# Audio tower on one core: the loads that lay out queries and keys move from SyncE's queue to GpSimd's

## Chip, cores and metric

The kernel runs on one core of a Trainium2 chip. The metric is the device time of one execution in microseconds, the median of the runs shown. The engines are TensorE (PE), ScalarE (ACT), VectorE (DVE), GpSimd (POOL) and SyncE (SP, which here only issues DMAs).

## What is computed

Eight waveforms of 120,000 samples are cut into frames of 80, so that each gives S = 1500 tokens of width D = 256. Each token goes through a layer of weights, a layer norm and an exact GELU, then through self attention with 16 heads of width 16 and a residual. In a last layer, tokens are routed to heads with an attention of their own, added, and normed once more; both kernels leave out this routed attention (its weights are no inputs of theirs) and compute the norm of that layer and its residual. What matters here:

```python
def proj(W, b):
    return (x @ W.T + b).reshape(B, S, H, hd).transpose(0, 2, 1, 3)
Q, K, V = (proj(Wq, bq), proj(Wk, bk), proj(Wv, bv))
scores = jnp.einsum('bhqd,bhkd->bhqk', Q, K) * scale
attn = jax.nn.softmax(scores, axis=-1)
out = jnp.einsum('bhqk,bhkd->bhqd', attn, V)
```

## The kernel before

**Units and periods.** The attention is done in 96 units, 12 to a batch: four groups of four heads, times three chunks of 500 queries. A unit has 24 periods, numbered from 0. In a period TensorE makes the scores of two heads for one tile of 125 keys (`scores`, L972), ScalarE takes their exponential as one instruction of 1000 columns (L537), and TensorE multiplies by the values in every second period (`attend`, L1002). The scores run one period ahead of the exponentials, in two pairs of PSUM banks. In each odd period TensorE also does one step of other work (`beside`): tokens of the next batch (`tok`), transposes (`turn`), projections to queries or keys (`qk`, four steps, L894), values (`val`), sums of squares (`norm`, L933), the test of the scores' range (`flag`) or the output projection (`out`, L924). The table PLAN names unit and period of each; NORMS names (4, 12), (5, 12) and (6, 8) for the layer norm of the next batch. Every engine walks the same loop over units and periods, and its instructions stand in that order; semaphores alone hold it in step with the others.

**The way of a projection.** A `qk` step number i (0 to 11 of a batch; even for queries, odd for keys) ends in PSUM. VectorE writes it as two halves of 16 bits into HL (L619, L621). `store_halves` sends HL to a scratch in HBM by one DMA on SP's queue (L281, 250 KB). GpSimd squares the upper half (`squares`, L426) for the range test. `lay_out` (L285 to L296) waits for the store (semaphore s_st) and issues eight DMAs of 62.5 KB on SP's queue (L295), which put the rows of the heads where the scores read them, in QA or KA. TensorE waits for all 48 DMAs of six projections (`laid_out`, on s_ld) before the first scores of unit 0 and of unit 6 of a batch, and these first scores stand in period 23 of the unit ahead. In the plan, projections end in period 9, 13 or 23; `lay_out` follows three periods after the store, so most of them stand in period 2 of the next unit.

**What else stands on SP's queue.** For the unit before, each unit issues three small steps: in period 1 `spread_sums` (thin<-Osb, L300), in period 7 `gather_sums` (Den<-thin, L304), in period 12 `store_attended` (oT<-Osb, L315). Between them VectorE inverts (L675) and multiplies (L679, L681). In period 13 come the loads of x and the stores of the output (out<-Y, L321, 500 KB).

**What stands on GpSimd.** `root1` (L402, L404) for the tokens, `root2` (L408, L410) and `add_bias` (four passes, L418) for the layer norm ahead of the projections, `squares` (L426), and `out_root` (L433 to L437) for the last layer norm. Who waits for them: VectorE for the roots, in `tok_norm` (L583), `norm_apply` (L600) and `finish_out` (L702, three periods after `take_out`); TensorE in `norm_sums`, which reads two squares and stands in period 3 of units 1, 3, 5, 7 and 9 and once in unit 10. The one in period 3 of unit 5 reads the squares of projections 10 and 11, and projection 11 ends in period 23 of unit 4.

Ahead of the first unit the same steps are done for six projections of batch 0, and `lay_out` follows each store on SP.

Of the kernel before, what the change touches and what calls it, by code (L numbers as in the profile page):

```python
# [5 lines left out]
def audio_tower(nc, x, tok_wT, tok_b, tok_g, tok_be, wqT, bq, wkT, bk, wvT, bv, woT, bo, ln_g, ln_b, out):  # L6
# [9 lines left out]
    HD = D // H  # L16
    QC = 500
    NC = S // QC
# [10 lines left out]
    WIN = NT * HG // 2  # L29
# [128 lines left out]
    with ExitStack() as ctx:  # L158
# [92 lines left out]
        def at(sem_, count):  # L251
            return count + TOTAL.get(sem_, 0) if second[0] else count
# [3 lines left out]
        def nth(b, i):  # L256
            return 12 * b + i

        def chunk_of(i):
            return i % (2 * NC) // 2  # L260
# [10 lines left out]
        def _(sp):  # L271
# [8 lines left out]
                sp.wait_ge(s_free, at(s_free, USE["qk", b, i] + 1))  # L280
                sp.dma_start(qk_s[b, i, :, :, :], HL[:, p % 3, :, :]).then_inc(s_st[p % 3], 16)  # L281

            def lay_out(b, i):  # L285
                p, k, w, m = nth(b, i), chunk_of(i), i % 2, i // (2 * NC)
                dst = KA if w else QA
                sp.wait_ge(s_st[p % 3], at(s_st[p % 3], 16 * (p // 3 + 1)))
                if p >= 4 * NC or second[0]:
                    sp.wait_ge(s_sc, at(s_sc, max(0, WIN * NC * 2 * (p // (2 * NC) - 1))))  # L290
                for par in range(2):
                    for blk in range(4):
                        to, half_ = 64 * par + HD * blk, blk // 2 if w else blk % 2
                        src = qk_s[b, i, :, half_, :].rearrange("(a two r) q -> two r a q", two=2, r=HD)
                        sp.dma_start(dst[to:to + HD, 2 * m:2 * m + 2, :, k * QC:(k + 1) * QC], src[par])\  # L295
                          .then_inc(s_ld, 16)  # L296

            def spread_sums(n):
                sp.wait_ge(s_ov, at(s_ov, n + 1))
                sp.dma_start(thin[:, :], Osb[HD:128:2 * HD, :].rearrange("j (s c) -> j s c", s=25)).then_inc(s_pk, 16)  # L300
# [22 lines left out]
            def run():  # L323
                load_x(1)
                for i in range(2 * NC):
                    store_halves(0, i)
                    if i > 0:
                        lay_out(0, i - 1)
                lay_out(0, 2 * NC - 1)
                stored = []  # L330
                for n in range(B * NU):
                    b, u = n // NU, n % NU
                    for k in range(WIN):
                        if stored and stored[0][0] == WIN * n + k:
                            lay_out(*stored.pop(0)[1:])
                        if k == TAKE and n > 0:
                            spread_sums(n - 1)
                        if k == INVERT and n > 0:
                            gather_sums(n - 1)
                        if k == NORMALISE and n > 0:  # L340
                            store_attended(n - 1)
                        if k == NORMALISE + 1:
                            if u == 4 and b + 2 < B:
                                load_x(b + 2)
                            if u in (1, 3, 6) and b > 0:
                                store_out(b - 1, u // 2 if u < 6 else 2)
                        for what, pb, i, step, last in pieces(b, u, k):
                            if what == "qk" and last:
                                store_halves(pb, i)
                                stored.append((WIN * n + k + 3, pb, i))  # L350
                spread_sums(B * NU - 1)
                gather_sums(B * NU - 1)
                store_attended(B * NU - 1)
                store_out(B - 1, 0)
                store_out(B - 1, 1)
                store_out(B - 1, 2)
# [27 lines left out]
        def _(pool):  # L384
# [27 lines left out]
            def add_bias(b, k):  # L412
                pool.wait_ge(s_z, at(s_z, b * NC + k + 1))
                if b == 0 and k == 0:
                    pool.wait_ge(s_wo, 16 * 5)
                for e in range(k * CT, k * CT + CT):
                    h = Hs[:, hslot(b, e), :]
                    ins = pool.tensor_tensor(h, h, b_o[:, :], ALU.add)  # L418
                ins.then_inc(s_hb, 1)

            def squares(b, i):
                p = nth(b, i)
                pool.wait_ge(s_free, at(s_free, USE["qk", b, i] + 1))
                if p >= 2:
                    pool.wait_ge(s_nm, at(s_nm, p // 2))
                pool.tensor_tensor(sq[:, p % 2, :], HL[:, p % 3, 0, :], HL[:, p % 3, 0, :], ALU.mult).then_inc(s_sq, 1)  # L426

            def out_root(b, e):
                n, k = b * NT + e, b * NC + e // CT
                if e % CT == 0 and k >= 2:  # L430
                    pool.wait_ge(s_yst[k % 2], at(s_yst[k % 2], 16 * (k // 2)))
                pool.wait_ge(s_free, at(s_free, USE["out", b, e] + 1))
                pool.tensor_tensor(Y[:, k % 2, e % CT, :], Hs[:, hslot(b, e), :], be_ln[:, :], ALU.add)  # L433
                pool.wait_ge(s_s1, at(s_s1, n + 1))
                pool.tensor_scalar(rs3[:, n % 2:n % 2 + 1], mv3[:, n % 2, 1:2], 1.0 + EPS, EPS * EPS, ALU.mult, ALU.add)
                pool.drain()
                pool.tensor_tensor(rs3[:, n % 2:n % 2 + 1], rs3[:, n % 2:n % 2 + 1], mhalf[0:T, 0:1], ALU.pow)\  # L437
                    .then_inc(s_r3, 1)

            def run():  # L440
                for i in range(NT // 2):
                    root1(0, i)
                    if i == 1 and not second[0]:
                        pool.wait_ge(s_top, 1)
                        pool.tensor_tensor(root[:, :], top[:, :], half[:, :], ALU.pow).then_inc(s_root, 1)
                root2(0, 0)
                for k in range(NC):
                    if k + 1 < NC:
                        root2(0, k + 1)
                    squares(0, 2 * k)  # L450
                    squares(0, 2 * k + 1)
                for k in range(NC):
                    add_bias(0, k)
                for b in range(B):
                    for u in range(NU):
                        for k in range(WIN):
                            if b + 1 < B and (u, k) in NORMS:
                                root2(b + 1, NORMS[u, k])
                                add_bias(b + 1, NORMS[u, k])
                            for what, pb, i, step, last in pieces(b, u, k):  # L460
                                if what == "tok" and last:
                                    root1(pb, i)
                                if what == "out" and last:
                                    out_root(pb, i)
                                if what == "qk" and last:
                                    squares(pb, i)
                for e in range(CT + 1, NT):
                    out_root(B - 1, e)

# [689 lines left out]
```

## Time and profile before

| | |
|---|---|
| median of 3 runs | 2360.52 us (2359.71 to 2369.72) |
| profiled execution | 2361.47 us |
| its span, first to last instruction | 2359.7 us |
| mean granted TensorE clock | 0.966 |
| busy: ACT / PE | 2134.5 us (90%) / 2080.5 us (88%) |
| busy: DVE / POOL | 963.5 us (41%) / 394.8 us (17%) |
| first exponential starts | 89.49 us |

The span is 1.8 us shorter than the execution's own time. ScalarE is busy for nine tenths of the span, and the exponentials are nearly all of that. A rise of time therefore shows as idle time of ScalarE between two exponentials. In the answers of the trace times are microseconds from the start of the span. A row of a timeline has start, duration, engine, line, operation, tiles, count, and in brackets the idle time of the engine ahead of it and what ended it.

### The profile page before, as it was taken

The numbers are of one execution on the slowest core, as the hardware profiler recorded it, in microseconds if no ns is written. First come the engines' busy times: TensorE is split into PE (matmuls) and PEld (weight loads), VectorE is DVE, ScalarE is ACT, GpSimd is POOL, SyncE is SP. The second block draws the span as 40 slices with busy tenths as digits, with TensorE's granted clock in tenths as the row PEclk, the third lists the DMA queues.
The fourth block names the chain that finished last, engine by engine and source line by source line (L and its number), as shares of the span: only waits on it lengthen the run. The fifth ranks groups of instructions, "written<-read, shape, count | busy, mean of one in ns | idle before, by whom it ended". The sixth has DMA issues, their size and how long they took to land.

```text
span 2359.7 us, 123320 instructions
## 1 busy us (share of the span) xinstructions
PE 2080.5 (88%) x56576; PEld 902.7 (38%) x56576; DVE 963.5 (41%) x2261; ACT 2134.5 (90%) x2334; POOL 394.8 (17%) x637
## 2 busy tenths in 40 slices
PE   4798999889998899988999799998999889999885
PEld 1432444333433344433444344443444333433223
DVE  6443335452344424444345433454335453343214
ACT  1498999989999899998999899998999989999993
POOL 2211102130122201222012210222102130011003
PEclk7998999999999999999999999999999999999997
DMA  2311211212121120221212112121211203122001
GB/s 71 81 45 42 56 42 46 56 31 75 32 57 48 44 67 22 59 64 43 62 25 57 53 48 58 35 58 38 66 41 48 53 23 78 28 58 57 18 10 35
DMA packets 114866, 113.91 MB, mean 48 GB/s; under 512 B 41003, under 2 KB 110698, under 8 KB 114338
## 3 DMA queue, kind: packets, MB, share of 16 engines
q1 hardware_dynamic: 111802, 104.10, 17.3%
q8 instruction: 446, 7.31, 1.3%
q10 hardware_dynamic: 2536, 1.83, 0.3%
q14 instruction: 82, 0.67, 0.1%
HBM read 55.16 MB, written 36.86 MB: 39 GB/s over the span
## 4 chain that ended last, share of the span: by engine, by line
ACT 40%; PE 27%; issue 13%; DVE 7%; SPq 5%; DMA 4%; POOL 2%; DVEq 2%; POOLq 0%
ACT prob L537 39%; PE PS L1002 12%; PE PS L972 7%; SPq L295 3%; DMA qk_halves_scratch<-HL 3%; PE PS L924 2%; SPq L315 1%; PE PS L871 1%; PE PS L909 1%; PE PS L894 1%; DMA oT<-Osb 1%; DVE Hs L576 1%; DVE z L600 1%; DVE Den L679 1%; POOL Hs L418 1%
## 5 line engine op out<-in xcount | busy, mean ns | idle before, releaser
L537 ACT ACTIVATE prob<-PS 125x1000 f32<-125x1000 f32 x2304 | 2089.7, 1070 | 155.9 <-PE PS L972 151.2
L1002 PE MATMUL PS<-prob,Vst 64*17 64x500 f32 (+1 forms) x18432 | 1214.7, 587 | 1.6 <-issue 0.8
L972 PE MATMUL PS<-QA,KA 64*32 64x500 f16 (+1 forms) x18432 | 958.9, 381 | 132.4 <-ACT prob L537 124.5
L972 PEld LDWEIGHTS PS<-QA,KA 64*32 64x32 f16 (+1 forms) x18432 | 276.8, 90 | 1054.0 <-ACT prob L537 1004.2
L1002 PEld LDWEIGHTS PS<-prob,Vst 61*17 61x17 f32 (+1 forms) x18432 | 341.3, 93 | 42.2 <-issue 9.0
L619 DVE TENSOR_SCALAR HL<-PS,b_qk 128x500 f16<-128x500 f32 x96 | 70.9, 739 | 459.4 <-PE PS L894 453.2
L894 PE MATMUL PS<-zT,w_qk 64*32 64x250 f32 x5760 | 229.4, 372 | 15.0 <-DVE Hs L576 8.5
L426 POOL TENSOR_TENSOR sq<-HL 128x500 bf16<-128x500 f16 x96 | 98.1, 1022 | 861.1 <-DVE HL L621 761.1
L924 PE MATMUL PS<-w_o,oT 64*32 64x128 f32 (+1 forms) x6144 | 129.9, 279 | 38.7 <-DVE Hs L576 27.9
L433 POOL TENSOR_TENSOR Y<-Hs,be_ln 125x256 f32<-125x256 f32 x96 | 70.3, 732 | 540.3 <-DVE Hs L688 529.5
L909 PE MATMUL PS<-w_v,zT 64*32 64x128 f32 (+1 forms) x5376 | 116.9, 280 | 34.2 <-DVE nrow L643 33.6
L894 PEld LDWEIGHTS PS<-zT,w_qk 64*32 64x32 f32 x5760 | 107.5, 106 | 70.8 <-DVE Hs L576 12.1
L924 PEld LDWEIGHTS PS<-w_o,oT 64*32 64x32 f32 (+1 forms) x6144 | 99.8, 108 | 88.6 <-DVE Hs L576 41.5
L909 PEld LDWEIGHTS PS<-w_v,zT 64*32 64x32 f32 (+1 forms) x5376 | 91.8, 109 | 66.2 <-DVE nrow L643 36.8
L688 DVE TENSOR_TENSOR Hs<-Hs,PS 125x256 f32<-125x256 f32 x96 | 40.3, 420 | 186.9 <-PE PS L924 186.9
L669 DVE COPY Osb<-PS 128x500 f32<-128x500 f32 x96 | 64.5, 672 | 117.9 <-PE PS L1002 116.4
L628 DVE TENSOR_TENSOR Vst<-PS,b_v 125x256 f32<-125x256 f32 x96 | 39.8, 419 | 160.4 <-PE PS L909 159.5
L871 PE MATMUL PS<-w_tok,X 40*32 40x256 f32 (+3 forms) x1536 | 68.2, 405 | 13.6 <-DMA w_tok<-in_tok_b 9.5
L418 POOL TENSOR_TENSOR Hs<-Hs,b_o 125x256 f32<-125x256 f32 x96 | 71.5, 775 | 31.4 <-DVE z L600 31.4
L675 DVE RECIPROCAL thin<-thin 100x20 f32<-100x20 f32 x96 | 26.5, 276 | 119.8 <-DMA thin<-Osb 119.8
L621 DVE SCALAR_TENSOR_TENSOR HL<-PS,b_qk,HL 128x500 f16<-128x500 f32 x96 | 71.0, 739 | 7.5 <-issue 0.4
L681 DVE TENSOR_TENSOR Osb<-Den,Osb 128x500 f32<-128x500 f32 x96 | 68.3, 712 | 7.5 <-issue 0.4
(83 smaller groups left out, 968.9 us busy)
## 6 DMA issues: line engine op xcount, KB each, us to landing
qk_halves_scratch<-HL SPq DMA_DIRECT2D x96, 250.0 KB, 2.3
QA<-qk_halves_scratch SPq DMA_DIRECT2D x384, 62.5 KB
KA<-qk_halves_scratch SPq DMA_DIRECT2D x384, 62.5 KB
oT<-Osb SPq DMA_DIRECT2D x384, 31.2 KB, 2.0
out<-Y SPq DMA_DIRECT2D x24, 500.0 KB
X<-in_x SPq DMA_DIRECT2D x16, 234.4 KB
thin<-Osb SPq DMA_DIRECT2D x96, 7.8 KB
Den<-thin SPq DMA_DIRECT2D x96, 7.8 KB
```

The lines of the kernel that those rows point to most:

```text
L295: sp.dma_start(dst[to:to + HD, 2 * m:2 * m + 2, :, k * QC:(k + 1) * QC], src[par])\
L418: ins = pool.tensor_tensor(h, h, b_o[:, :], ALU.add)
L426: pool.tensor_tensor(sq[:, p % 2, :], HL[:, p % 3, 0, :], HL[:, p % 3, 0, :], ALU.mult).then_inc(s_sq, 1)
L537: act.activation(prob[0:T, 2 * (w % 6):2 * (w % 6) + 2, :], PS[0:T, 2 * (w % 2):2 * (w % 2) + 2, 0:QC], ACT.Exp, scale=scl)\
L619: dve.tensor_scalar(hi, both, bias, None, ALU.add)
L621: dve.scalar_tensor_tensor(out=lo, in0=both, scalar=bias, in1=hi, op0=ALU.add, op1=ALU.subtract)\
L871: last = pe.matmul(PS[lo:hi, bank + j, 0:D], X[rows, 2 * i + j, lo:hi], w_tok[rows, :], start=(step == 0), stop=(step == 1))
L894: last = pe.matmul(PS[lo:hi, bank + j, 0:QC // 2], w_qk[rows, c, w, m * 128 + lo:m * 128 + hi], zT[rows, c, k * QC + j * QC // 2:k * QC + ...
L909: last = pe.matmul(PS[lo:hi, bank + j, 0:D // 2], zT[rows, c, t + lo:t + hi], w_v[rows, c, j * D // 2:(j + 1) * D // 2], start=(step == 0 ...
L924: last = pe.matmul(PS[lo:hi, bank + j, 0:D // 2], oT[rows, c, oslot(b, e // CT), e % CT * T + lo:e % CT * T + hi], w_o[rows, c, j * D // 2 ...
L972: last = pe.matmul(PS[lo:hi, bank, 0:QC], KA[rows, G % NG, h // 2, t * T + lo:t * T + hi], QA[rows, G % NG, h // 2, c * QC:(c + 1) * QC], ...
L1002: last = pe.matmul(PS[lo:lo + HD + 1, bank + r, 0:QC], Vst[rows, b % 2, t, g * HG + j, :], prob[rows, (HG * t + j) % 12, :], start=(t == 0 ...
```

## The change

`lay_out` is the same function with the same eight DMAs and the same waits, but it stands in GpSimd's program and issues on GpSimd's own queue. SP's program loses it. Its place in GpSimd's order: ahead of the first unit, after the two squares of each chunk; later in period 13 (`NORMALISE + 1`), ahead of that period's other pieces, where all projections that were stored so far and are not yet laid out are taken. A projection that ends in period 23 is thus laid out in period 13 of the next unit, one that ends in period 9 in period 13 of the same unit, and one that ends in period 13 of unit 6 in period 13 of unit 7.

```diff
@@ SyncE
-            def lay_out(b, i):
-                ...
-                sp.wait_ge(s_st[p % 3], at(s_st[p % 3], 16 * (p // 3 + 1)))
-                ...
                 for i in range(2 * NC):
                     store_halves(0, i)
-                    if i > 0:
-                        lay_out(0, i - 1)
-                lay_out(0, 2 * NC - 1)
-                stored = []
...
-                        if stored and stored[0][0] == WIN * n + k:
-                            lay_out(*stored.pop(0)[1:])
...
-                                stored.append((WIN * n + k + 3, pb, i))
@@ GpSimd
+            def lay_out(b, i):
+                p, k, w, m = nth(b, i), chunk_of(i), i % 2, i // (2 * NC)
+                dst = KA if w else QA
+                pool.wait_ge(s_st[p % 3], at(s_st[p % 3], 16 * (p // 3 + 1)))
+                if p >= 4 * NC or second[0]:
+                    pool.wait_ge(s_sc, at(s_sc, max(0, WIN * NC * 2 * (p // (2 * NC) - 1))))
+                for par in range(2):
+                    for blk in range(4):
+                        to, half_ = 64 * par + HD * blk, blk // 2 if w else blk % 2
+                        src = qk_s[b, i, :, half_, :].rearrange("(a two r) q -> two r a q", two=2, r=HD)
+                        pool.dma_start(dst[to:to + HD, 2 * m:2 * m + 2, :, k * QC:(k + 1) * QC], src[par])\
+                          .then_inc(s_ld, 16)
...
                     squares(0, 2 * k)
                     squares(0, 2 * k + 1)
+                    lay_out(0, 2 * k)
+                    lay_out(0, 2 * k + 1)
...
                         for k in range(WIN):
+                            if k == NORMALISE + 1:
+                                while stored:
+                                    lay_out(*stored.pop(0))
                             if b + 1 < B and (u, k) in NORMS:
...
                                 if what == "qk" and last:
                                     squares(pb, i)
+                                    stored.append((pb, i))
```

The lines of the changed kernel are numbered anew: its `squares` is L404, `root2` is L386 and L388, `add_bias` L396, `out_root` L426 to L430 and the DMAs of `lay_out` L418. On SP the store of HL is still L281, the spread, gather and attended DMAs are L285, L289 and L300.

**GpSimd ahead of the first unit**, before (sq is the tile of squares, rs of the roots, Hs of the tokens):

```order
L426 TENSOR_TENSOR sq<-HL 128x500 x2
L408 TENSOR_SCALAR rs<-mv 125x4
L410 TENSOR_TENSOR rs<-rs,mhalf 125x4
L426 TENSOR_TENSOR sq<-HL 128x500 x4
L418 TENSOR_TENSOR Hs<-Hs,b_o 125x256 x12
```

and now:

```order
L404 TENSOR_TENSOR sq<-HL 128x500 x2
L418 DMA QA<-qk_halves_scratch 16x4x500 x8
L418 DMA KA<-qk_halves_scratch 16x4x500 x8
L386 TENSOR_SCALAR rs<-mv 125x4
L388 TENSOR_TENSOR rs<-rs,mhalf 125x4
L404 TENSOR_TENSOR sq<-HL 128x500 x2
L418 DMA QA<-qk_halves_scratch 16x4x500 x8
L418 DMA KA<-qk_halves_scratch 16x4x500 x8
L404 TENSOR_TENSOR sq<-HL 128x500 x2
L418 DMA QA<-qk_halves_scratch 16x4x500 x8
L418 DMA KA<-qk_halves_scratch 16x4x500 x8
L396 TENSOR_TENSOR Hs<-Hs,b_o 125x256 x12
```

All 48 DMAs now stand on GpSimd, 16 of them ahead of the root of the third chunk's norm, and the squares lie between them.

**GpSimd in units 4 and 5 of a batch**, from the norm in period 12 of unit 4 to the end of the one in unit 5, now (without the two rows of DMAs it is the order before, with the other line numbers):

```order
L386 TENSOR_SCALAR rs<-mv 125x4
L388 TENSOR_TENSOR rs<-rs,mhalf 125x4
L396 TENSOR_TENSOR Hs<-Hs,b_o 125x256 x4
L418 DMA QA<-qk_halves_scratch 16x4x500 x8
L404 TENSOR_TENSOR sq<-HL 128x500
L426 TENSOR_TENSOR Y<-Hs,be_ln 125x256
L428 TENSOR_SCALAR rs<-mv 125x1
L430 TENSOR_TENSOR rs<-rs,mhalf 125x1
L386 TENSOR_SCALAR rs<-mv 125x4
L388 TENSOR_TENSOR rs<-rs,mhalf 125x4
L396 TENSOR_TENSOR Hs<-Hs,b_o 125x256 x4
L418 DMA KA<-qk_halves_scratch 16x4x500 x8
```

The first eight DMAs (projection 10) stand between the bias of unit 4 and the square of projection 11; the second eight (projection 11) behind the bias of unit 5.

**SP around the start of unit 7**, before:

```order
L281 DMA qk_halves_scratch<-HL 128x1000
L295 DMA QA<-qk_halves_scratch 16x4x500 x8
L281 DMA qk_halves_scratch<-HL 128x1000
L300 DMA thin<-Osb 100x1x20
L295 DMA KA<-qk_halves_scratch 16x4x500 x8
L304 DMA Den<-thin 4x25x20
L315 DMA oT<-Osb 16x500 x4
```

and now:

```order
L281 DMA qk_halves_scratch<-HL 128x1000 x2
L285 DMA thin<-Osb 100x1x20
L289 DMA Den<-thin 4x25x20
L300 DMA oT<-Osb 16x500 x4
```

The second store and the two DMAs of the sums no longer have sixteen DMAs and two waits for stores among them.

## Rows read from the trace of the kernel before

**Rows 1.** The page, its first part: busy time, share, instructions of each engine.
```profile
PE 2080.5 (88%) x56576; PEld 902.7 (38%) x56576; DVE 963.5 (41%) x2261; ACT 2134.5 (90%) x2334; POOL 394.8 (17%) x637
```

**Rows 2.** Groups by line: count | busy us, mean ns | idle before, releaser.
```profile
L537 ACT ACTIVATE prob<-PS 125x1000 f32<-125x1000 f32 x2304 | 2089.7, 1070 | 155.9 <-PE PS L972 151.2
```

**Rows 3.** The page, DMA issues: count, KB of each, us to landing.
```profile
qk_halves_scratch<-HL SPq DMA_DIRECT2D x96, 250.0 KB, 2.3
```

**Rows 4.** Timeline of SP's queue, the loads of one projection, unit 4.
```profile
461.77 3.59 SPq L295 DMA_DIRECT2D QA<-qk_halves_scratch  x8
```

**Rows 5.** Timeline ahead of the first unit: POOL, then SP, then PE.
```profile
52.77 1.12 POOL L426 TENSOR_TENSOR sq<-HL 128x500 bf16<-128x500 f16 x1 [1.54 <-DVE HL L621]
59.30 0.22 POOL L408 TENSOR_SCALAR rs<-mv 125x4 f32<-125x4 f32 x1 [5.41 <-DVE mv L594]
59.67 1.03 POOL L410 TENSOR_TENSOR rs<-rs,mhalf 125x4 f32<-125x4 f32 x1
...
83.24 3.70 SPq L295 DMA_DIRECT2D KA<-qk_halves_scratch  x8
...
88.81 1.03 PE L972 MATMUL PS<-QA,KA 64*32 64x500 f16 x16 [7.57 <-DMA KA<-qk_halves_scratch]
```

**Rows 6.** Timeline of POOL, end of unit 4 and unit 5 of batch 1.
```profile
483.50 2.99 POOL L418 TENSOR_TENSOR Hs<-Hs,b_o 125x256 f32<-125x256 f32 x4 [1.50 <-DVE z L600]
488.02 1.02 POOL L426 TENSOR_TENSOR sq<-HL 128x500 bf16<-128x500 f16 x1 [1.52 <-DVE HL L621]
...
505.32 2.77 POOL L418 TENSOR_TENSOR Hs<-Hs,b_o 125x256 f32<-125x256 f32 x4 [1.50 <-DVE z L600]
```

**Rows 7.** Timeline of PE in unit 5 of batch 1.
```profile
489.33 0.39 PE L933 MATMUL PS<-sq,head_sel 128*32 128x500 bf16 x2
...
505.42 1.11 PE L909 MATMUL PS<-w_v,zT 64*32 64x128 f32 x32 [5.10 <-DVE nrow L643]
...
514.82 0.40 PE L972 MATMUL PS<-QA,KA 64*32 64x500 f16 x8
```

**Rows 8.** Timeline of ACT, units 5 to 7 of batch 1.
```profile
506.99 1.00 ACT L537 ACTIVATE prob<-PS 125x1000 f32<-125x1000 f32 x1 [5.50 <-PE PS L972]
509.07 1.01 ACT L537 ACTIVATE prob<-PS 125x1000 f32<-125x1000 f32 x1 [1.08 <-PE PS L972]
510.34 1.00 ACT L537 ACTIVATE prob<-PS 125x1000 f32<-125x1000 f32 x1 [0.27 <-PE PS L972]
511.80 35.31 ACT L537 ACTIVATE prob<-PS 125x1000 f32<-125x1000 f32 x39 [0.46 <-PE PS L972]
548.53 7.60 ACT L537 ACTIVATE prob<-PS 125x1000 f32<-125x1000 f32 x8 [1.42 <-PE PS L972]
558.07 77.55 ACT L537 ACTIVATE prob<-PS 125x1000 f32<-125x1000 f32 x86 [1.94 <-PE PS L972]
```

**Rows 9.** Busy time by stretch: stretch, us, PE, PEld, DVE, ACT, POOL, clock, DMA share, GB/s.
```profile
505.00:511.00 6.00, 5.58 (x120) 3.35 (x128) 3.31 (x10) 2.67 (x3) 2.77 (x4) 0.50 0.01 3
```

**Rows 10.** Timeline, unit 0 of batch 1: SP, POOL, DVE.
```profile
380.60 5.36 SPq L295 DMA_DIRECT2D QA<-qk_halves_scratch  x8
...
382.55 0.73 POOL L433 TENSOR_TENSOR Y<-Hs,be_ln 125x256 f32<-125x256 f32 x1 [3.14 <-DVE Hs L688]
...
384.02 0.56 POOL L437 TENSOR_TENSOR rs<-rs,mhalf 125x1 f32<-125x1 f32 x1
...
389.31 0.74 DVE L619 TENSOR_SCALAR HL<-PS,b_qk 128x500 f16<-128x500 f32 x1 [4.21 <-PE PS L894]
```

**Rows 11.** Timeline of SP and DVE in unit 7 of batch 1.
```profile
532.38 0.35 SPq L281 DMA_DIRECT2D qk_halves_scratch<-HL  x1
539.68 4.66 SPq L295 DMA_DIRECT2D QA<-qk_halves_scratch  x8
...
546.86 0.28 DVE L675 RECIPROCAL thin<-thin 100x20 f32<-100x20 f32 x1 [5.21 <-DMA thin<-Osb]
...
555.30 0.01 DVE L679 LOAD_MASK_SELECT Den<-Den  x1 [4.50 <-DMA Den<-thin]
```

More of the change, by code:

```diff
@@ L281, in store_halves @@
                 sp.dma_start(qk_s[b, i, :, :, :], HL[:, p % 3, :, :]).then_inc(s_st[p % 3], 16)
-            def lay_out(b, i):
-                p, k, w, m = nth(b, i), chunk_of(i), i % 2, i // (2 * NC)
-                dst = KA if w else QA
-                sp.wait_ge(s_st[p % 3], at(s_st[p % 3], 16 * (p // 3 + 1)))
[L289 to L296, printed above, removed]
             def spread_sums(n):
@@ L451, in run @@
                     squares(0, 2 * k + 1)
+                    lay_out(0, 2 * k)
+                    lay_out(0, 2 * k + 1)
                 for k in range(NC):
                     add_bias(0, k)
+                stored = []
                 for b in range(B):
```

## Prediction, made before the change ran

> **What bounds the kernel now.** The page's first part comes first: ScalarE is busy for 90% of the span and TensorE for 88%, GpSimd for 17% [rows 1]. The groups by line then say what ScalarE does: 2304 exponentials make 2089.7 us, and nearly all its 155.9 us of idle time ends with scores of TensorE [rows 2]. So only what opens or closes a gap between two exponentials changes the time, plus what moves the first of them. SP's queue and GpSimd sit on that path only where something waits for them. The timelines show four such places, and the change touches each of them.
>
> **What one moved DMA costs.** No row shows a DMA issued from GpSimd. On SP eight of them take 3.59 us at the least [rows 4], 4.66 us often [rows 11], 5.36 us at the most of these rows [rows 10]: 0.45, 0.58 and 0.67 us each. That is the price from below. From above I take the 2.3 us from a store's issue to its landing [rows 3], as if GpSimd were held until the data is there. Between them I take **1.02 us**, the square of 500 columns, the dearest thing that GpSimd does over and over in the rows [rows 6]; a program on its cores has to write these descriptors, so I hold a full GpSimd instruction nearer than SP's 0.58 us. Eight make 8.16 us. Everything below hangs on this price c, and steeply.
>
> **The start.** TensorE's first scores wait until 88.81 us for the last KA load [rows 5]. SP issued it by 86.94 (83.24 + 3.70), so landing takes 1.87 us more. Now GpSimd ends its second square at 53.89 [rows 5] and from there is never idle: 48 DMAs (48.96), the root of the third chunk (0.22 + 1.03, some 1.4 with the drain between) and four squares (4.1). With the landing that is 53.89 + 48.96 + 1.4 + 4.1 + 1.87 = 110.2, against 88.81: **+21.4 us**. The third chunk's projections come later too, since their norm waits for the root behind 16 DMAs, but they are ready long before GpSimd asks for them.
>
> **Unit 5, period 3.** In batch 1 the bias of unit 4 ends at 486.49 and the square of projection 11 starts at 488.02 [rows 6]; TensorE reads it at 489.33 [rows 7]. Now projection 10's eight DMAs stand between: they run to 494.65, the square to 495.67, and TensorE stands 6.34 us in `norm_sums`, with the next scores behind it. Such a stall is in the trace already: TensorE waits 5.10 us at 505.42 [rows 7], and ScalarE loses 5.50 + 1.08 + 0.27 + 0.46 = 7.31 us [rows 8], for behind the wait the granted clock is 0.50, the 1.2 GHz level, over 6 us [rows 9]. I carry the surplus of 2.2 us over: 8.5 us. Batch 0 has no output projections in its unit 4, so its bias is done early; the last batch has no bias. 6 x 8.5 = **+51 us**.
>
> **The end of unit 5.** Projection 11's DMAs now start behind the bias, at 508.09 (505.32 + 2.77) [rows 6], end at 516.25 and have landed at 518.12. TensorE made the first scores of unit 6 at 514.82 [rows 7]. It is 3.3 us late, with the clock 5.5 us, in all eight batches (the last has no bias there, but an output root about as late): **+44 us**. The other half of the batch is safe: projections 4 and 5 are laid out in units 9 and 10, a unit and more ahead of their use.
>
> **Units 0 to 2.** Projection 6's store has landed at 380.60 [rows 10]; eight DMAs run to 388.76. `out_root`, which ran from 382.55 to 384.58 [rows 10], with the gap in it 1.7 us of work, ends at 390.5. VectorE stands in `finish_out` for it and takes projection 7 some 1.7 us after the 389.31 of before [rows 10]; its squares and sums are what TensorE wants in period 3. Units 1 and 2 have the same pattern with about 1 us less. I put down 2 us a batch for seven batches, **+14 us**. In unit 3 the last token root comes some 7 us late, but it has until the GELU in period 2 of the next unit, and I put it down at nothing; at a dearer c that cover would be gone.
>
> **What SP gives back.** In unit 7 SP waits for a slow store (issued 532.38, landed 539.68), then issues eight loads, and only then takes the next store and the sums: VectorE waits 5.21 and 4.50 us for thin and Den [rows 11], ScalarE 1.42 and 1.94 us [rows 8]. Without `lay_out` both waits go. Batch 1 is the worst; over six batches the gaps in this unit sum to some 10 us, and exponentials after a gap overlap less: **-12 us**. Elsewhere SP's relief is worth nothing. In unit 5 Den comes late as well, but VectorE was not waiting for it: it was at the output of period 11, and the 5.10 us stall is VectorE's own chain to the range test. That stall stays. The transfers themselves move the same bytes and stay hidden behind the exponentials; their cover is the slack until unit 6 or 12, which is what the unit 5 term takes away.
>
> **Sum.** 21.4 + 51 + 44 + 14 - 12 = +118 us on the profiled execution's 2361.5 us, 1 us over the median of the runs. I predict **2480 us**.
>
> **Rivals.**
> - *Issuing from GpSimd is cheap: faster.* If GpSimd only hands the DMA on, at 0.2 us or so, the eight before the square take 1.6 us, which the 2.8 us between bias and sums hides; the loads of unit 5 land in time; at the start the last loads follow the last store at once, some 6 us earlier; unit 7 gives its 12 to 15 us. That is about 2342 us. It decides from c below 0.35 us. For it: GpSimd is idle for 83% of the span, and SP's issue of a store takes 0.35 us [rows 11]. Against it: SP needs 0.45 to 0.67 us with nothing else to do. The Trainium skill ("DMA: Bandwidth & Descriptors", on the anatomy of a DMA on the GpSimd path) states a rule that leads here: descriptor generation is "small, variable", and most of a DMA's fixed cost is the wait for the write's receipt, which would not hold GpSimd. No row of this trace shows that path. Chance 0.06.
> - *As cheap as on SP, 0.4 to 0.64 us.* At 0.58 the start is even (53.9 + 27.8 + 7.4 = 89.1), the square is 2.8 us late, with the clock's loss up to 5, and unit 6's scores are in time: 0 + 17 to 30 - 12, or 2367 to 2380 us; over the whole span of prices 2353 to 2386 us. Chance 0.10.
> - *Dearer, above 1.3 us.* At 1.3: start +35, unit 5 period 3 6 x 10.8, its end 8 x 7.7, units 0 to 2 now 12 us a batch since every out root stalls VectorE: +234, 2595 us. At 2.3 us the same sum is near 2950 us. The skill has a rule for this side ("SBUF — State Buffer", on the trap that VectorE blocks DMA): while VectorE runs a copy or scalar pass in its two-port mode, GpSimd cannot write descriptors, so DMAs issued there stall until it ends. Which of VectorE's passes here would do so no row tells. Chance 0.15.
> - *My reading, 0.64 to 1.3 us*, 2386 (at 0.64: +3 + 33 + 0 + 0 - 12) to 2595 us. Chance 0.69.
>
> **Numbers.** The range 2370 to 2640 us leaves out the cheap issue, part of the second case, and prices above some 1.4 us. A measurement of this kernel can tell about 0.5%, 12 us, from no change. Faster by more needs c below 0.35 us: 0.06. Within it lies c from 0.35 to 0.55 us: 0.06. Slower: 0.88.
>
> **What would show it.** The gap before ACT's first exponential ends near 111 us. GpSimd's queue shows eight DMAs in about 8 us; a PE row of the sums of squares in unit 5 waits 6 us for the square; the first scores of unit 6 wait about 3 us for KA; unit 7's waits for thin and Den are gone. If eight DMAs take under 4.5 us, the forecast is wrong by its price; if they take 8 us and these waits are missing, by its mechanism; if `out_root` rows carry most of the loss, my 2 us a batch was too small.

## The result and the profile after

| | before | after |
|---|---|---|
| median of the runs, us | 2360.11 (4 runs, 2358.67 to 2369.72) | 2396.32 (4 runs, 2389.17 to 2400.67) |
| ratio after/before, 95% interval | | 1.0142 [1.0101, 1.0182] |
| profiled execution, us (span) | 2361.5 (2359.7) | 2400.67 (2398.9) |
| idle of ScalarE before its exponentials, us | 155.9 | 191.2 |

The change is slower, as forecast, and the time lies in the range; but it costs 36 us, not 118. The ratio here and below is the one on record with the run; it is not the quotient of the two medians and differs from it by up to 0.24%. First the page: the busy time of each engine, the queues (packets, MB, share of the 16 DMA engines), and three groups of instructions by line (busy us, mean ns | idle before them and what ended it).

```profile
PE 2098.4 (87%) x56576; PEld 904.4 (38%) x56576; DVE 963.0 (40%) x2261; ACT 2136.2 (89%) x2334; POOL 785.0 (33%) x1405
...
q0 software_dynamic: 24576, 49.20, 9.0%
q1 hardware_dynamic: 50362, 54.90, 7.7%
...
L537 ACT ACTIVATE prob<-PS 125x1000 f32<-125x1000 f32 x2304 | 2091.4, 1072 | 191.2 <-PE PS L972 186.4
...
L418 POOL DMA_DIRECT2D QA<-qk_halves_scratch x384 | 196.8, 520 | 19.5 <-DMA qk_halves_scratch<-HL 19.3
L418 POOL DMA_DIRECT2D KA<-qk_halves_scratch x384 | 195.7, 517 | 10.7 <-DMA qk_halves_scratch<-HL 10.6
```

The 768 DMAs now stand as busy time of GpSimd: 196.8 + 195.7 = 392.5 us, or **0.511 us each** (the rows' own means, 520 and 517 ns, count the slight overlap of neighbours twice), half of the 1.02 us that I took, and inside SP's own 0.45 to 0.67 us [rows 4, 10, 11]. The exponentials' busy time has hardly moved against [rows 2]; their gaps have grown by 35 us. The waits of the trace (us in total, times, longest) say who stands for GpSimd now:

```profile
POOL rs L382 <- issue: 55.8, 24, 6.3
POOL rs L430 <- issue: 51.4, 42, 4.1
...
DVE Y L702 <- POOL rs L430: 105.6, 61, 7.1
DVE Hs L583 <- POOL rs L382: 76.5, 48, 8.3
...
PE PS L933 <- POOL sq L404: 15.0, 6, 2.9
PE PS L972 <- DMA KA<-qk_halves_scratch: 11.1, 5, 5.8
```

The last two rows are waits that I forecast, for the square and for KA; they are small, and 5.8 us of the KA row is the wait of the start. The first four I did not. Lines 382 and 430 are the second halves of `root1` and `out_root`, and "issue" says that GpSimd waited there for nothing that the profile shows. In the code one thing stands between the halves, `pool.drain()`. Before, VectorE waited 11.7 us in all for `root1` and 29.9 us for `out_root`; now it is 76.5 and 105.6 us.

To see where this reaches ScalarE, I cut the span into units, from the first exponential of a unit to the first of the next, and summed the differences to before over the eight batches. This and the tables below are worked out from the records of the 2304 exponentials, and are good to some 0.2 us:

| us | start | unit 1 | unit 4 | unit 5 | unit 7 | unit 11 | the rest | sum |
|---|---|---|---|---|---|---|---|---|
| after − before | +3.0 | +3.0 | +2.5 | **+22.6** | **−13.0** | **+21.5** | −0.4 | +39.2 |

**The start.** GpSimd's timeline (start, duration, line, operation, count [idle before it]):

```profile
54.50 4.26 POOL L418 DMA_DIRECT2D QA<-qk_halves_scratch  x8
58.75 4.03 POOL L418 DMA_DIRECT2D KA<-qk_halves_scratch  x8
62.80 0.24 POOL L386 TENSOR_SCALAR rs<-mv 125x4 f32<-125x4 f32 x1
65.83 1.04 POOL L388 TENSOR_TENSOR rs<-rs,mhalf 125x4 f32<-125x4 f32 x1 [2.79 <-issue]
...
81.81 4.06 POOL L418 DMA_DIRECT2D QA<-qk_halves_scratch  x8 [1.74 <-DMA qk_halves_scratch<-HL]
```

Eight DMAs take 4.03 to 4.26 us, the first exponential begins at 92.5 us instead of 89.5, and the root of the third chunk stands 2.79 us in its drain.

**Unit 5, period 3, batch 1.** GpSimd, then TensorE, then ScalarE, then the window of 499 to 505 us (busy time and count of each engine, PEclk the granted clock):

```profile
490.99 2.98 POOL L396 TENSOR_TENSOR Hs<-Hs,b_o 125x256 f32<-125x256 f32 x4 [1.50 <-DVE z L600]
493.92 4.13 POOL L418 DMA_DIRECT2D QA<-qk_halves_scratch  x8
498.06 1.03 POOL L404 TENSOR_TENSOR sq<-HL 128x500 bf16<-128x500 f16 x1
```

```profile
499.24 0.60 PE L933 MATMUL PS<-sq,head_sel 128*32 128x500 bf16 x2 [2.43 <-POOL sq L404]
```

```profile
500.46 1.00 ACT L537 ACTIVATE prob<-PS 125x1000 f32<-125x1000 f32 x1 [2.47 <-PE PS L972]
502.54 1.00 ACT L537 ACTIVATE prob<-PS 125x1000 f32<-125x1000 f32 x1 [1.08 <-PE PS L972]
504.12 1.00 ACT L537 ACTIVATE prob<-PS 125x1000 f32<-125x1000 f32 x1 [0.57 <-PE PS L972]
505.80 2.96 ACT L537 ACTIVATE prob<-PS 125x1000 f32<-125x1000 f32 x3 [0.68 <-PE PS L972]
```

```profile
499.00:505.00 6.00, 5.76 (x62) 1.85 (x70) 1.68 (x4) 2.89 (x3) 0.09 (x1) 0.50 0.04 10
```

This is the chain of the forecast, step by step: bias, eight DMAs, square, TensorE late, then 6 us at a granted clock of 0.50, the 1.2 GHz level. Only its size differs: TensorE waits 2.43 us, not 6.34, and ScalarE loses 2.47 + 1.08 + 0.57 + 0.68 = 4.80 us.

**Unit 11, batch 1.** GpSimd, VectorE, TensorE and ScalarE around a `root1`:

```profile
618.39 4.06 POOL L418 DMA_DIRECT2D KA<-qk_halves_scratch  x8 [1.39 <-DMA qk_halves_scratch<-HL]
642.54 0.23 POOL L380 TENSOR_SCALAR rs<-mv 125x2 f32<-125x2 f32 x1 [20.09 <-DVE mv L570]
646.87 0.72 POOL L382 TENSOR_TENSOR rs<-rs,mhalf 125x2 f32<-125x2 f32 x1 [4.09 <-issue]
```

```profile
647.63 0.88 DVE L583 SCALAR_TENSOR_TENSOR Hs<-Hs,rs,be_tok 125x256 f32<-125x256 f32 x2 [4.21 <-POOL rs L382]
```

```profile
649.03 0.66 PE L871 MATMUL PS<-w_tok,X 41*32 41x256 f32 x16 [1.92 <-DVE Hs L688]
...
654.72 0.67 PE L924 MATMUL PS<-w_o,oT 64*32 64x128 f32 x32 [2.06 <-DVE Hs L576]
```

```profile
649.95 3.85 ACT L537 ACTIVATE prob<-PS 125x1000 f32<-125x1000 f32 x4 [1.70 <-PE PS L972]
655.75 1.00 ACT L537 ACTIVATE prob<-PS 125x1000 f32<-125x1000 f32 x1 [1.95 <-PE PS L972]
657.84 1.00 ACT L537 ACTIVATE prob<-PS 125x1000 f32<-125x1000 f32 x1 [1.08 <-PE PS L972]
```

The last DMA was done at 622.45 us. GpSimd then idled for 20 us, and still the drain between 642.77 and 646.87 took 4.1 us. It is the first drain since the one in period 8 of unit 6; the loads of projections 0 to 5, all 48 of them, were issued between, in units 7 to 10, where no root is due. Sorting all gaps between the halves of a root by what lies before them gives a pattern: 0.15 us with no DMA since the last drain, 0.82 to 0.83 us behind 8 that had landed, 4.08 to 4.09 us behind 48, and 1.3 to 6.3 us in 29 cases where the loads' last packet was still to come, as in the row of 65.83 us above: there the drain began at 63.04 us, the last packet was done at 64.31, and the drain ended at 65.83. In all 29 the drain ends 0.8 to 2.5 us after that packet. The first three fit 0.17 + 0.082 us per DMA issued since the last drain.

So there were two theories for the 39 us. **A:** the issues cost 0.51 us each, and move the time only where they stand ahead of a square (unit 5); the drains behind them cost the rest (unit 11, unit 1, part of the start); unit 7's gain comes from the relieved order of SP. **B:** the new queue and the transfers on it are what costs (packets, contention, landing), or the gain in unit 7 needs the second queue.

### The profile page after: what moved, and what is told of

It reads as the page before. It is cut to its first block, busy times and chain, and to the rows that moved or that the text cites. A ratio compares the mean times of both kernels' runs of the same rounds, so it can differ in the third digit from the quotient of the medians.

```text
span 2398.9 us, 123320 instructions
## 1 busy us (share of the span) xinstructions
PE 2098.4 (87%) x56576; PEld 904.4 (38%) x56576; DVE 963.0 (40%) x2261; ACT 2136.2 (89%) x2334; POOL 785.0 (33%) x1405
## 3 DMA queue, kind: packets, MB, share of 16 engines
q0 software_dynamic: 24576, 49.20, 9.0%
q1 hardware_dynamic: 50362, 54.90, 7.7%
## 4 chain that ended last, share of the span: by engine, by line
ACT 36%; PE 30%; issue 16%; POOL 7%; DVE 5%; DMA 2%; DVEq 2%; POOLq 1%; SPq 0%
ACT prob L537 36%; PE PS L1002 14%; PE PS L972 8%; PE PS L924 2%; POOL KA L418 2%; POOL QA L418 2%; PE PS L909 2%; POOL Hs L396 1%; DMA qk_halves_scratch<-HL 1%; PE PS L894 1%; PE PS L880 1%; PE PS L871 1%; DMA KA<-qk_halves_scratch 1%; POOL rs L388 1%; DVE Hs L576 1%
## 5 line engine op out<-in xcount | busy, mean ns | idle before, releaser
L537 ACT ACTIVATE prob<-PS 125x1000 f32<-125x1000 f32 x2304 | 2091.4, 1072 | 191.2 <-PE PS L972 186.4
L404 POOL TENSOR_TENSOR sq<-HL 128x500 bf16<-128x500 f16 x96 | 98.0, 1021 | 550.0 <-DVE HL L621 507.1
L426 POOL TENSOR_TENSOR Y<-Hs,be_ln 125x256 f32<-125x256 f32 x96 | 70.8, 737 | 461.6 <-DVE Hs L688 461.3
L418 POOL DMA_DIRECT2D QA<-qk_halves_scratch x384 | 196.8, 520 | 19.5 <-DMA qk_halves_scratch<-HL 19.3
L418 POOL DMA_DIRECT2D KA<-qk_halves_scratch x384 | 195.7, 517 | 10.7 <-DMA qk_halves_scratch<-HL 10.6
L924 PE MATMUL PS<-w_o,oT 64*32 64x128 f32 (+1 forms) x6144 | 131.0, 279 | 40.3 <-DVE Hs L576 29.9
L909 PE MATMUL PS<-w_v,zT 64*32 64x128 f32 (+1 forms) x5376 | 115.4, 277 | 31.5 <-DVE nrow L643 31.5
L909 PEld LDWEIGHTS PS<-w_v,zT 64*32 64x32 f32 (+1 forms) x5376 | 90.7, 108 | 61.6 <-DVE nrow L643 34.6
L702 DVE SCALAR_TENSOR_TENSOR Y<-hg,rs,Y 125x256 f32<-125x256 f32 x96 | 52.0, 541 | 108.7 <-POOL rs L430 105.6
L380 POOL TENSOR_SCALAR rs<-mv 125x2 f32<-125x2 f32 x48 | 10.8, 224 | 250.8 <-DVE mv L570 250.3
L871 PE MATMUL PS<-w_tok,X 40*32 40x256 f32 (+3 forms) x1536 | 67.2, 410 | 25.4 <-DVE Hs L688 11.5
## 6 DMA issues: line engine op xcount, KB each, us to landing
QA<-qk_halves_scratch POOLq DMA_DIRECT2D x384, 62.5 KB
KA<-qk_halves_scratch POOLq DMA_DIRECT2D x384, 62.5 KB
oT<-Osb SPq DMA_DIRECT2D x384, 31.2 KB
```

The costliest lines, as they stand in the source:

```text
L418: pool.dma_start(dst[to:to + HD, 2 * m:2 * m + 2, :, k * QC:(k + 1) * QC], src[par])\
L537: act.activation(prob[0:T, 2 * (w % 6):2 * (w % 6) + 2, :], PS[0:T, 2 * (w % 2):2 * (w % 2) + 2, 0:QC], ACT.Exp, scale=scl)\
L871: last = pe.matmul(PS[lo:hi, bank + j, 0:D], X[rows, 2 * i + j, lo:hi], w_tok[rows, :], start=(step == 0), stop=(step == 1))
L909: last = pe.matmul(PS[lo:hi, bank + j, 0:D // 2], zT[rows, c, t + lo:t + hi], w_v[rows, c, j * D // 2:(j + 1) * D // 2], start=(step == 0 ...
L924: last = pe.matmul(PS[lo:hi, bank + j, 0:D // 2], oT[rows, c, oslot(b, e // CT), e % CT * T + lo:e % CT * T + hi], w_o[rows, c, j * D // 2 ...
```

## The experiments

Each ratio is against runs of the kernel before on the same chip, with its 95% interval. "By unit" is the table's measure above.

**1. The late place on SP's own queue.** The kernel before, with the loads in period 13, still issued by SP.

```diff
                     for k in range(WIN):
-                        if stored and stored[0][0] == WIN * n + k:
-                            lay_out(*stored.pop(0)[1:])
 ...
                         if k == NORMALISE + 1:
+                            while stored:
+                                lay_out(*stored.pop(0))
 ...
-                                stored.append((WIN * n + k + 3, pb, i))
+                                stored.append((pb, i))
```

> The loads go back to SP's queue, but keep the new place in period 13. Theory A (the loss of the change comes from GpSimd's order and its drains, the gain in unit 7 from leaving period 2 of SP): no loss in units 5 and 11, the start as before, the 13 us of unit 7 kept: some 2347 us, 13 us under the kernel before. Theory B (the loss in units 5 and 11 comes from the later time of the loads, whatever the queue): units 5 and 11 lose some 40 us here too, near 2390 us.

Measured: 2351.61 us (before 2360.51), ratio 0.9938 [0.9915, 0.9961], a little faster (0.9962 by the medians). Unit 7 gains 13.5 us, as much as with GpSimd's queue, so that gain is of the order, not of the queue. Unit 5 (−1.9) and unit 11 (+0.7) show no loss without GpSimd. Unit 2 loses 7.8 us. Its timelines in batch 2, SP's queue (the window opens behind the first of the eight loads) and then VectorE:

```profile
684.02 4.39 SPq L295 DMA_DIRECT2D KA<-qk_halves_scratch  x7
688.45 0.34 SPq L321 DMA_DIRECT2D out<-Y  x1
688.84 0.34 SPq L281 DMA_DIRECT2D qk_halves_scratch<-HL  x1
689.91 0.61 SPq L300 DMA_DIRECT2D thin<-Osb  x1
```

```profile
696.53 0.28 DVE L675 RECIPROCAL thin<-thin 100x20 f32<-100x20 f32 x1 [6.65 <-DMA thin<-Osb]
```

The small `thin` DMA, issued behind the loads and two stores (500 and 250 KB), comes to VectorE only 6 us after its issue. Over the kernel VectorE's waits for `thin` are 156.0 us in 74 waits, longest 7.3, where the kernel before has 119.8 and 5.2, and the changed one 101.7 and 2.4. Here, then, the second queue is worth something; that this wait is what costs unit 2 its 7.8 us is read from the trace, and no run took it away.

**2. One drain more, where nobody waits.** The changed kernel with a `pool.drain()` in unit 10, ahead of unit 11's roots.

```diff
+                            if (u, k) == (10, 20):
+                                pool.drain()
```

> The change, with one more drain on GpSimd in period 20 of unit 10, where it is idle. Theory A (the first drain behind GpSimd's DMAs costs about 0.08 us for each DMA issued since the last drain, 4.1 us for 48): the 4.1 us move to the new drain, the gap in the token root of unit 11 shrinks to 0.15 us, unit 11 gives back its 21 us: some 2376 us. Theory B (the wait in unit 11 is that root's own, after a long idle time, or the transfers'): the gap of 4.1 us and the 2396 us stay.

Measured: 2368.4 us, ratio 1.0033 [1.002, 1.0045]; unit 11 is at 0.0 us (with the change +21.5), unit 7 at −12.4, unit 5 at +16.3. GpSimd's timeline where the change had its 4.09 us:

```profile
611.02 4.05 POOL L418 DMA_DIRECT2D KA<-qk_halves_scratch  x8 [1.66 <-DMA qk_halves_scratch<-HL]
634.70 0.23 POOL L380 TENSOR_SCALAR rs<-mv 125x2 f32<-125x2 f32 x1 [19.62 <-DVE mv L572]
635.09 0.72 POOL L382 TENSOR_TENSOR rs<-rs,mhalf 125x2 f32<-125x2 f32 x1 [0.16 <-issue]
```

An added instruction takes 28 us off the changed kernel: the price is paid once, by the first drain behind the DMAs, and unit 10 has cover for it. The loads themselves did not change. That unit 5 came out 6 us better as well, which makes the total 8 us lower than expected, no run explains.

**3. The loads before the square.** The changed kernel with the loads at period 2 of the next unit.

```diff
-                            if k == NORMALISE + 1:
+                            if k == 2:
```

> The change, with the loads on GpSimd in period 2 of the next unit instead of period 13, so behind the square of period 23 and ahead of the bias of period 12. Theory A (unit 5 loses because eight DMAs stand ahead of the square of projection 11 and eight behind the bias): unit 5 gives back its 22 us, unit 11 keeps its loss: some 2374 us. Theory B (unit 5 loses by transfers of GpSimd's queue beside the store and the sums): unit 5 stays 3 to 4 us a batch longer than before, near 2396 us.

Measured: 2411.85 us, ratio 1.0215 [1.0194, 1.0236]. The part on unit 5 held: from +22.6 to −4.9 us. The total missed by 38 us, since unit 1 went from +3.0 to +34.6. GpSimd, VectorE and ScalarE in unit 1 of batch 1:

```profile
395.82 4.12 POOL L418 DMA_DIRECT2D QA<-qk_halves_scratch  x8
399.93 4.03 POOL L418 DMA_DIRECT2D KA<-qk_halves_scratch  x8
403.98 0.74 POOL L426 TENSOR_TENSOR Y<-Hs,be_ln 125x256 f32<-125x256 f32 x1
...
406.91 0.56 POOL L430 TENSOR_TENSOR rs<-rs,mhalf 125x1 f32<-125x1 f32 x1 [1.93 <-issue]
```

```profile
407.50 0.48 DVE L702 SCALAR_TENSOR_TENSOR Y<-hg,rs,Y 125x256 f32<-125x256 f32 x1 [5.30 <-POOL rs L430]
```

```profile
411.58 1.00 ACT L537 ACTIVATE prob<-PS 125x1000 f32<-125x1000 f32 x1 [5.27 <-PE PS L972]
```

Two projections are laid out together there, 8.15 us ahead of an output root that VectorE needs at once. A unit has its own free place in GpSimd's queue; one period does not suit them all.

**4. No drain.** The changed kernel, where the first half of a root raises a semaphore and the second waits for it; the same in `root2` and `out_root`.

```diff
-                pool.tensor_scalar(rs1[:, p, :], mv1[:, p, :, 1], EPS, None, ALU.add)
-                pool.drain()
+                pool.tensor_scalar(rs1[:, p, :], mv1[:, p, :, 1], EPS, None, ALU.add).then_inc(s_own, 1)
+                owned[0] += 1
+                pool.wait_ge(s_own, owned[0])
```

> The change, with the drains between the two halves of each root replaced by a wait on a semaphore that the first half raises. Theory A (the drain waits for GpSimd's DMAs, an ordinary instruction behind them doesn't): the gaps of 0.8 to 6.3 us in the roots go, unit 11 gives back 21 us, some 2375 us. Theory B (GpSimd itself is not free for the next instruction after DMAs): gaps of 4.1 us stay in unit 11 with the semaphore, 2396 us.

Measured: 2366.54 us, ratio 1.0026 [1.0012, 1.004]. Unit 11 −0.7, unit 1 −1.0, start −3.4, unit 5 +21.4, unit 7 −13.4, and +3.6 after the last exponential. The second half of `root1`, and the loads beside it (groups by line):

```profile
L424 POOL DMA_DIRECT2D QA<-qk_halves_scratch x384 | 196.9, 520 | 27.6 <-issue 13.9 <-DMA qk_halves_scratch<-HL 13.7
...
L388 POOL TENSOR_TENSOR rs<-rs,mhalf 125x2 f32<-125x2 f32 x48 | 34.4, 717 | 4.0
```

The idle time before it is 4.0 us over 48 roots, where the changed kernel has 59.3, and each gap is 0.08 us, less even than a drain with no DMA before it (0.15). The loads cost GpSimd what they did. So 2396.32 − 2366.54 = 29.8 us of the changed kernel's time are drains (27 us by the two ratios, 1.0142 and 1.0026; the four runs of the changed kernel lie within 11.5 us). What is left against before is unit 5's +21.4 less unit 7's 13.4, and smaller terms. Unit 5's sum has parts of both signs, by period: +22.9 us in periods 4 to 7, behind the sums of squares, +8.0 in the last period, at the first scores of unit 6, and −9.4 in periods 16 to 19, behind the stall at L909 (L915 here).

**5. Both causes mended.** As 4; projections 10 and 11 are both laid out in period 2 of unit 5, behind the square of projection 11. In the change, 10 comes in period 13 of unit 4, ahead of that square, and 11 in period 13 of unit 5, behind the bias.

```diff
-                            if k == NORMALISE + 1:
+                            if k == (2 if u == 5 else NORMALISE + 1) and u != 4:
```

> The kernel with the semaphore in place of the drains, and with projections 10 and 11 laid out by GpSimd in period 2 of unit 5, behind the square of projection 11 and ahead of the bias of unit 5. Theory A (what is left of the loss is the order on GpSimd in unit 5 alone): the 21 us of unit 5 go, the 13 us of unit 7 stay: some 2345 us, under both kernels. Theory B (GpSimd's own queue of DMAs has a cost of its own in unit 5): 2366 us as with the semaphore alone.

Measured: **2341.65 us** (6 runs, 2340.03 to 2342.6), before 2357.0; ratio 0.9937 [0.9919, 0.9954]. Unit 5 −9.6, unit 7 −13.0, unit 11 +0.2, start −1.1. The exponentials' row against [rows 2]:

```profile
L543 ACT ACTIVATE prob<-PS 125x1000 f32<-125x1000 f32 x2304 | 2085.9, 1076 | 136.6 <-PE PS L978 132.9
```

Their gaps are 136.6 us, 19 less than before and 55 less than with the change. TensorE no longer waits for a square at all. This is the lowest time found: the same 768 DMAs on GpSimd's queue, with the drains away and one place moved. Against its own runs of the kernel before, though, it is no better than run 1 by the ratios on record (0.9937 and 0.9938; the medians give 0.9935 and 0.9962), and run 1 left the loads on SP; so these runs do not settle whether GpSimd's queue is the better place.

**6. The price doubled.** As 4, with every load cut into two DMAs of half the size, 16 for a projection, the same bytes. At 0.51 us a piece this gives the forecast's price of 1.02 us per original DMA by another way.

```diff
-                        pool.dma_start(dst[to:to + HD, 2 * m:2 * m + 2, :, k * QC:(k + 1) * QC], src[par])\
-                          .then_inc(s_ld, 16)
+                        for g in range(2):
+                            pool.dma_start(dst[to:to + HD, 2 * m + g, :, k * QC:(k + 1) * QC],
+                                           src[par][:, 2 * g:2 * g + 2, :]).then_inc(s_ld, 16)
```

> The kernel with the semaphore in place of the drains, and each DMA of the loads cut into two of 31 KB, 16 to a projection. If GpSimd's price is per DMA (0.51 us), eight loads cost it 8.2 us, which is the price that the forecast assumed: by its own sum (start +21, unit 5 +51 and +44, units 0 to 2 +14, unit 7 -12) 2480 us. If the price goes by bytes or rows, a projection costs 4.1 us as before and the time stays near 2366 us.

Measured: 2481.08 us (before 2357.0), ratio 1.0534 [1.0509, 1.0559]. By unit: start +19.3, unit 1 +11.7, unit 3 +15.7, unit 5 +72.2, unit 6 +8.1, unit 7 −13.1, the rest +5.8. Groups by line, GpSimd in unit 5 of batch 1, and VectorE in unit 3 of batch 2:

```profile
L425 POOL DMA_DIRECT2D QA<-qk_halves_scratch x768 | 384.8, 509 | 44.7 <-issue 31.0
L425 POOL DMA_DIRECT2D KA<-qk_halves_scratch x768 | 383.4, 507 | 11.9 <-DMA qk_halves_scratch<-HL 11.9
```

```profile
511.95 8.04 POOL L425 DMA_DIRECT2D QA<-qk_halves_scratch  x16
520.01 1.03 POOL L410 TENSOR_TENSOR sq<-HL 128x500 bf16<-128x500 f16 x1
```

```profile
756.33 0.49 DVE L709 SCALAR_TENSOR_TENSOR Y<-hg,rs,Y 125x256 f32<-125x256 f32 x1 [8.45 <-POOL rs L437]
```

768.2 us for 1536 DMAs are 0.500 us each: half the bytes cost nearly the same, so GpSimd is held per DMA, not per byte. (The packets on its queue doubled with the DMAs, from 24576 to 49152, 32 to a DMA in both; so a price per packet can't be told from one per DMA, here or for the drains in run 7.) And a projection that holds it for 8.04 us gives 2481.08 us, where the forecast had 2480; against its own runs of the kernel before, it is 124 us more, where the forecast had 118. That the total is so close is partly luck, as the terms below show; but the path of the forecast, from price to time, is borne out.

**7. The price of the drain doubled.** The changed kernel, drains and all, with the loads cut in two. Its time is that of a single execution.

> The change itself, with its drains, and each DMA of the loads cut into two. If the first drain behind DMAs costs 0.08 us for each DMA issued since the last drain, the gap in the first token root of unit 11 is 0.17 + 96 x 0.082, about 8.0 us, and the one in unit 6, behind 16 landed DMAs, 1.5 us. If it costs by bytes or is a fixed time, they stay at 4.1 and 0.83 us.

Measured: 2626.52 us. GpSimd in unit 11 of batch 1 and in unit 2 after it:

```profile
705.68 0.23 POOL L380 TENSOR_SCALAR rs<-mv 125x2 f32<-125x2 f32 x1 [16.13 <-DVE mv L571]
713.92 0.72 POOL L382 TENSOR_TENSOR rs<-rs,mhalf 125x2 f32<-125x2 f32 x1 [8.01 <-issue]
...
722.14 0.71 POOL L382 TENSOR_TENSOR rs<-rs,mhalf 125x2 f32<-125x2 f32 x1 [0.16 <-issue]
```

Behind 96 DMAs the drain takes 8.01 us, and the next one 0.16. Behind 16 that have landed it takes 1.48 us. With 0.82 for 8 and 4.09 for 48 that is one line through four counts, with the bytes of a projection held: a drain on GpSimd costs some 0.17 + 0.082 us per DMA that it issued since the drain before. Against 6, the same loads without drains, the drains cost some 145 us, by that one execution.

**8. One of unit 5's two moves.** As 4, with projection 10 alone at period 2 of unit 5; 11 stays in period 13, behind the bias.

```diff
-                            if k == NORMALISE + 1:
-                                while stored:
+                            if k == NORMALISE + 1 and u != 4 or (u, k) == (5, 2):
+                                while stored and not ((u, k) == (5, 2) and stored[0][1] == 11):
```

> The kernel with the semaphore, and only projection 10 laid out in period 2 of unit 5, projection 11 still behind the bias. Theory A: the stall of the sums of squares in period 3 of unit 5 goes (14 us over the batches), the late first scores of unit 6 (gaps of 0.7 to 2.2 us, 7 us in all) stay: some 2353 us. If unit 5 keeps its 21 us, the stall has another cause.

Measured: 2347.64 us, ratio 0.9961 [0.9948, 0.9973]; unit 5 at 0.0. By period this is 0.0 us in periods 4 to 7, where run 4 has +22.9, so that stall goes with projection 10's place alone; −4.6 in periods 16 to 19 (run 4 −9.4); and +4.8 in the last period (run 4 +8.0), the late first scores of unit 6, which stay, as expected. Run 5, which moves 11 as well, has 0.0, −9.5 and 0.0. Of its 9.6 us more, half are those scores; the other half stands in periods 16 to 19, and no run explains it. This version, too, is a little faster than the kernel before, by 0.4%.

## Why the prediction was right or wrong

**The step that failed is "Between them I take 1.02 us".** I priced a DMA from GpSimd like its dearest full instruction; it costs 0.511 us, as SP's do. The bounds of 0.45 and 2.3 us held; the choice within them was wrong, and I gave the case "as cheap as on SP" a chance of 0.10. For this price the forecast had "2367 to 2380 us", and run 4, which has the issues without the drains, took 2366.54 us. Run 6 doubles the price and took 2481.08 us against my 2480. So the price alone is worth 2481.08 − 2366.54 = 115 us too much (118 us, if each is taken against its own runs of the kernel before).

**What was missing is the drain.** My sum held the drain between two halves at what it had cost before. Run 4 shows 29.8 us for it, and 115 − 30 = 85 us is then the miss, 2480 − 2396; since run 6 came out at the forecast, that this adds up is no further proof. The question was there to be asked: the code shows a drain behind the loads, and a step that is moved to a queue must be looked at with everything on that queue that waits for it to be empty. It wasn't in the rivals either.

Term by term, with run 6 as the forecast's own price:

| term | forecast at 1.02 us | run 6 (1.00 us, no drain) | after (0.51 us, drains) |
|---|---|---|---|
| start | +21.4 | +19.3 | +3.0 |
| unit 5, periods 4 to 7, behind the sums of squares | +51 | +50.5 | +23.2 |
| unit 5, periods 16 to 19 | 0 | −5.9 | −6.9 |
| last period of unit 5, and unit 6 | +44 | +27.7 + 8.1 | +6.6 + 0.7 |
| units 0 to 3 | +14 | +28.8 | +2.4 |
| unit 7 | −12 | −13.1 | −13.0 |
| unit 11 | 0 | −0.6 | +21.5 |
| behind the last exponential | 0 | +3.8 | −0.4 |

*The start* was right: the first exponential comes when GpSimd's DMAs let it. With 0.511 us in my own sum it is 53.89 + 24.5 + 7.4 = 85.8 against 88.81, or −3.0 us, and run 4 has −3.4; the drains make it +3.0. *Unit 5, period 3* was right in every link, and in size at the forecast's price. *Its end* was right in kind but too dear: 35.8 us at that price where I had 44, and in the changed kernel the first scores of unit 6 are late in five batches only, by 0.33 to 2.31 us. *Periods 16 to 19 of unit 5* I had at nothing ("elsewhere SP's relief is worth nothing"). TensorE's 5.0 us wait at L909 does stay in six batches, as I said, but it falls from 3.02 to 1.25 us in batch 0, and the gaps behind it are shorter in several others; run 1, on SP's own queue, has 5.2 us less there too. Why is not known. *Units 0 to 3* at the forecast's price cost twice what I put down. The late token root that I put at nothing is not the reason: it would show in unit 4, which is only 1.3 us longer in run 6. It is `out_root` once more: in the row of 756.33 us VectorE waits 8.45 us for the root of unit 2, which stands behind sixteen issues, and TensorE then waits 3.20 us for HL in unit 3. So the pattern that I priced at 2 us a batch costs about 4 at that price. These errors cancel in the total of 2481. *Unit 7* was right, in its place and size, for the reason given: run 1 gets the same 13.5 us on SP's own queue.

**The two rivals of the price.** The Trainium skill, "DMA: Bandwidth & Descriptors" (the anatomy of a DMA on the GpSimd path), calls descriptor generation "small, variable". GpSimd was held 0.511 us by busy time over count, and the record of one issue of the QA loads is 0.512 us at the least and in the median, 0.727 at the most: hardly variable, and too much for the cheap rival, which needed less than 0.35 us. What the same page of the Trainium skill says of the write's receipt fits the trace: the issues of 58.75 us end at 62.78, and their last packet is done only at 64.31. The Trainium skill, "SBUF — State Buffer" (the trap that VectorE blocks DMA), led to the dearer rival; with a longest issue of 0.727 us among 768, beside a VectorE busy for 40% of the span, no such stall shows in this case. Whether any pass of VectorE here runs in the mode that it speaks of, no row tells.

**What stays open.** Why a drain costs 0.08 us for each DMA long landed is not known, only that it does so by their number (or that of their packets). The +3.6 us behind the last exponential in the versions with the semaphore were not looked into. Whether the late place of run 1, with `thin` ahead of the loads, would bring SP's own queue to the 2341.65 us of run 5 was not tried.

## What to carry to other kernels

Before moving DMAs to an engine that also computes, look at its program for drains behind them: much of the bill came from there, not from the issues alone, and a semaphore of its own in the drain's place took that part away. Price an issue per DMA, not per byte, and ask at each place what work stands next in that queue; here eight DMAs a batch cost some 23 us over the batches ahead of one square and nothing behind it. Try the new order on the old queue as well: the 13 us that this change gains in unit 7 were to be had without the move.

## What was unexpected of the hardware

- A drain on GpSimd costs time for DMAs that have long landed: 0.82, 1.48, 4.09 and 8.01 us behind 8, 16, 48 and 96 DMAs, the last two after 20 and 16 us of idleness; where loads had not landed, it ended 0.8 to 2.5 us after their last packet and took up to 6.3 us. The next drain is back at 0.16 us.
- An issue from GpSimd takes 0.511 us for 62.5 KB and 0.500 us for 31.2 KB (busy time by count).
- The same loads made 24576 packets on GpSimd's queue. On SP's queue they had made 61440, by the difference of that queue's packets, 111802 before and 50362 after; the busy share of the 16 DMA engines on the two queues together went from 17.3% to 9.0 + 7.7 = 16.7%. So fewer and larger packets saved next to nothing in the engines' time.
